# One windowed-attention kernel: transposed scores by tiles of keys, one slot later, with 8 KB stack rows loaded in three pieces

## The chip, the cores and the metric

The kernel runs on one core of one Trainium2 chip. The metric is the device time of one execution in microseconds (us). Below, PE is TensorE, DVE is VectorE, ACT is ScalarE, POOL is GpSimd and SP is SyncE, which here only issues transfers. "L786" is line 786 of the kernel before.

## The reference

Input `x` is 4 batches of 1024 tokens of width 256.

```python
h = layernorm(x) * (1 + ca) + sa                  # ca, sa, ... from silu(c) @ wmod, one row per batch
q, k, v = split(h @ qkv_w + qkv_b)                # 16 heads of 16
scores = q @ k.T / 4; allowed: 0 < key distance <= 128 (and key >= 0)
local = softmax(scores) @ v                       # a window of 128 keys before each query
rq = h @ rq_w + rq_b; rk, rv = split(mean over 16 tokens of h @ rkv_w + rkv_b)   # 4 latent heads
remote = softmax(rq @ rk.T / 4, earlier latents only) @ rv @ rout_w + rout_b
gate = sigmoid(local @ gl_w + remote @ gr_w)      # per head
x1 = x + ga * ((gate * local + (1 - gate) * remote) @ out_w + out_b)
h2 = layernorm(x1) * (1 + cb) + sb
out = x1 + gb * (layernorm(h2 + outs) * ln_g + ln_b)   # outs: attention over routed tokens
```

Both kernels, before and changed, leave out `outs` and compute `layernorm(h2)`; the change does not touch that branch.

## The kernel before

**Tiles and slots.** The 4096 tokens are 32 tiles of 128 (`NT = 32`), 8 to a batch (`NB = 8`). Every engine runs `slot(n)` for n = 0 to 34, and a slot works on several tiles at once, one stage each: A (layer norm and transpose) for tile n+4, P (projection of q or k for a pair of tiles) for n+3, Q (split into terms, stack) for n+2, K (v and latent projections) for n+1, S (scores by query rows, for the row maximum) for n, T (transposed scores, exp, mask, times v) for n-1, C (gate, output projection) for n-2, D (second branch, store) for n-3. The order inside a slot is written out by hand per engine in its `slot` function, and semaphores do the rest. On PE a slot opens with the transpose of the maxima at L786.

**Score precision and the stack.** q and k are float32 values that are split into three bf16 terms each. Six products of terms are summed by the matmul itself: `qst` holds, for each head, 6 blocks of 16 rows (terms 0,0,0,1,1,2 of q), `kst` the matching ones of k (terms 0,1,2,0,1,0), 96 rows in all. Rows 96 to 111 hold minus the row maximum (in `qst`) and a one-hot of the head (in `kst`), so that the transposed scores come out with the maximum already taken off. `shift` (ACT, L574) writes those 16 rows of `qst` for a tile.

**How a stack is made.** For a pair of tiles, the even tile's turn makes q and the odd tile's turn makes k. ACT, POOL, ACT, POOL compute the terms (`part1`, `res1`, `part2`, `part3`), then SP stores them to a DRAM scratch (`store_terms`, L345) and loads the stack back in 6 transfers of 16 partitions, 128 KB each (`load_stack`, L361), in pieces of 512 bytes. In slot n the terms are those of tile n+2, and the pair is first used by `scores` in the next even slot. So the k stack is stored and loaded in an odd slot and needed when the even slot after it starts: PE waits for `stack_loaded` at the head of `scores(t, 1)`, `t` even.

**SP's order.** In an odd slot SP issues: store of k terms, k stack loads, store of y. In an even slot: store of q terms, store of y (it waits for DVE's last operation of tile n-3), q stack loads. After slots 0, 2 and 4 it also issues 1 MB of `x` for the next batch (`load_batch`); `x_all` holds all of x.

**Transposed scores.** For query tile m = n-1 and each head, `scores_t` (L797, L798) runs two matmuls: queries of m against the keys of tile m-1 (not for a batch's first tile) and against those of m. Each loads its 128 keys as weights. ACT exponentiates two heads at a time (`exps`, L583), POOL masks four heads at a time (L432 own keys, L436 previous keys), and `sum_v` multiplies by v.

**Shared banks.** `project_v` (L731) writes the PSUM bank `p_qkv` that `shift` reads, and waits for it:

```python
pe.wait_ge(shift_ready, done(t - 2))
```

## Time and profile before

| | |
|---|---|
| median of 3 runs | 607.0 us (604.92 to 607.2) |
| the profiled execution's own time | 606.81 us |
| its span, first to last instruction | 605.1 us |
| busy: PE, DVE, ACT, POOL | 497.0, 433.6, 354.5, 378.3 us |
| mean granted clock of TensorE | 0.924 |
| packets of SP's transfer queue | 90428, 52.58 MB |

The span is what the trace accounts for; the 1.7 us around it lie outside. A change of 0.5% (3 us) is about what the measurement can tell. A matmul's own duration includes its way through the array, so the spacing of starts, not the duration, tells what a stream of matmuls costs.

### The profile page before, as it was taken

How to read it: one execution, taken by the hardware profiler on the slowest of the kernel's cores; microseconds unless marked ns; L12 is line 12 of the kernel's file. 1: busy time of each engine (PE TensorE's matmuls, PEld its weight loads, DVE VectorE, ACT ScalarE, POOL GpSimd, SP SyncE). 2: the span in 40 equal slices, each digit the busy share in tenths (PEclk: the TensorE clock that was granted, in tenths of full speed). 3: DMA queues.
4: the chain of work that ended last, by engine and by line, in shares of the span. 5: the costliest groups of instructions: out<-in, count | busy, mean ns of one | idle time of the engine just before them, and what ended most of it. 6: DMA issues, size and time to landing. Idle time of an engine off the chain costs nothing.

```text
span 605.1 us, 19951 instructions
## 1 busy us (share of the span) xinstructions
PE 497.0 (82%) x7168; PEld 373.3 (62%) x7168; DVE 433.6 (72%) x1193; ACT 354.5 (59%) x868; POOL 378.3 (63%) x516
## 2 busy tenths in 40 slices
PE   2547789897899979898989799998999798989771
PEld 2305567675677657676767577776776576756440
DVE  2255556787688868787879687886888786876645
ACT  1111467667477657676676657776776676654640
POOL 2313246777377647777777666775777575766652
PEclk9966899899799989999999988998999998997875
DMA  8487957529254755556282819183656565460000
GB/s 268 103 134 233 170 85 124 116 44 163 41 111 67 103 74 89 89 74 105 42 110 54 124 43 127 37 117 60 90 88 90 88 89 90 58 95 11 10 10 18
DMA packets 93388, 55.16 MB, mean 91 GB/s; under 512 B 8916, under 2 KB 91500, under 8 KB 93292
## 3 DMA queue, kind: packets, MB, share of 16 engines
q1 hardware_dynamic: 90428, 52.58, 51.3%
q10 hardware_dynamic: 2864, 1.31, 1.0%
q8 instruction: 59, 0.97, 0.8%
q14 instruction: 37, 0.30, 0.2%
HBM read 37.07 MB, written 16.80 MB: 89 GB/s over the span
## 4 chain that ended last, share of the span: by engine, by line
PE 67%; issue 16%; POOL 7%; DVE 4%; DMA 2%; ACTq 1%; SPq 1%; ACT 1%; POOLq 0%; DVEq 0%
PE p_qkv L721 9%; PE p_pv L810 8%; PE p_qkv L731 7%; PE p_misc L877 5%; PE p_x L776 5%; PE p_y L797 4%; PE p_x L769 4%; PE p_y L798 4%; PE p_a L742 2%; PE p_a L822 2%; PE p_misc L860 2%; PE p_qkv L851 2%; PE p_a L707 2%; PE p_a L744 2%; POOL pr L432 2%
## 5 line engine op out<-in xcount | busy, mean ns | idle before, releaser
L583 ACT ACTIVATE pr<-p_y 128x512 f32<-128x512 f32 x224 | 124.6, 595 | 66.1 <-PE p_y L798 63.8
L1150 DVE TENSOR_REDUCE mtok<-p_x 128x3 bf16<-128x480 f32 (+1 forms) x192 | 109.3, 585 | 60.5 <-PE p_x L776 54.3
L460 POOL TENSOR_TENSOR dif<-local,rem 128x272 f32<-128x272 f32 x32 | 30.9, 965 | 111.8 <-DVE local L1188 111.8
L432 POOL TENSOR_SCALAR_AFFINE_SELECT pr<-pr 128x512 f32<-128x512 f32 x128 | 89.6, 701 | 11.4 <-ACT pr L585 8.8
L442 POOL TENSOR_TENSOR rstd<-ve,half 128x1 f32<-128x1 f32 x96 | 58.3, 607 | 49.5 <-DVE ve L1070 49.4
L436 POOL TENSOR_SCALAR_AFFINE_SELECT pr<-pr 128x512 f32<-128x512 f32 x112 | 81.9, 731 | 0.0
L797 PE MATMUL p_y<-qst,kst 112*128 112x128 bf16 x448 | 67.2, 222 | 7.7 <-ACT pr L583 4.8
L798 PE MATMUL p_y<-qst,kst 112*128 112x128 bf16 x512 | 73.4, 221 | 0.0
L721 PE MATMUL p_qkv<-hT,wqk 128*128 128x256 f32 x256 | 67.7, 411 | 2.2 <-DVE qkf L1102 1.3
L810 PE MATMUL p_pv<-pr,vp 128*18 128x128 f32 x1920 | 68.4, 284 | 1.2 <-POOL pr L432 0.7
L769 PE MATMUL p_x<-edge,ident_bf 128*32 128x192 bf16 (+1 forms) x672 | 43.8, 250 | 28.5 <-issue 28.5
L810 PEld LDWEIGHTS p_pv<-pr,vp 128*18 128x18 f32 x1920 | 48.8, 101 | 19.4 <-POOL pr L436 9.6
L731 PE MATMUL p_qkv<-wv,hT 128*128 128x272 f32 x128 | 46.0, 491 | 18.0 <-issue 18.0
L574 ACT ACTIVATE qst<-p_qkv 16x2048 bf16<-16x2048 bf16 x32 | 59.8, 1870 | 0.8
L776 PE MATMUL p_x<-kst,qst 96*32 96x160 bf16 x1792 | 60.1, 238 | 0.0
L591 ACT ACTIVATE oT<-p_pv 128x512 f32<-128x512 f32 x32 | 19.1, 597 | 67.0 <-PE p_pv L810 67.0
L798 PEld LDWEIGHTS p_y<-qst,kst 112*128 112x128 bf16 x512 | 49.1, 99 | 10.2 <-issue 1.8
L721 PEld LDWEIGHTS p_qkv<-hT,wqk 128*128 128x128 f32 x256 | 49.4, 203 | 9.7 <-issue 2.2
L797 PEld LDWEIGHTS p_y<-qst,kst 112*128 112x128 bf16 x448 | 43.2, 99 | 17.9 <-issue 8.0
L416 POOL TENSOR_TENSOR qkf<-qkf,terms 128x512 f32<-128x512 f32 x32 | 40.2, 1258 | 18.2 <-ACT terms L562 18.1
L769 PEld LDWEIGHTS p_x<-edge,ident_bf 128*32 128x32 bf16 x672 | 17.9, 94 | 52.0 <-issue 43.7
L423 POOL TENSOR_TENSOR terms<-qkf,terms 128x512 bf16<-128x512 f32 x32 | 37.1, 1160 | 10.8 <-ACT terms L568 10.8
(131 smaller groups left out, 1104.5 us busy)
## 6 DMA issues: line engine op xcount, KB each, us to landing
qst<-scr_q SPq DMA_DIRECT2D x96, 128.0 KB, 4.8
kst<-scr_k SPq DMA_DIRECT2D x96, 128.0 KB, 4.4
scr_q<-terms SPq DMA_DIRECT2D x16, 384.0 KB, 2.8
scr_k<-terms SPq DMA_DIRECT2D x16, 384.0 KB, 6.4
out_y<-y SPq DMA_DIRECT2D x32, 128.0 KB, 2.0
x_all<-in_x SPq DMA_DIRECT2D x3, 1024.0 KB, 8.9
pr<-in_wmod SPq DMA_DIRECT2D x1, 1024.0 KB, 9.0
x_all<-in_x SPq DMA_DIRECT2D x1, 768.0 KB, 5.4
```

The lines of the kernel that those rows point to most:

```text
L432: ins = pool.affine_select(out=own, in_=own, compare_op=ALU.is_ge, fill=0.0, base=-1, pattern=[[0, 4], [1, P]], channel_multiplier=-1)
L436: ins = pool.affine_select(out=prev, in_=prev, compare_op=ALU.is_ge, fill=0.0, base=-1, pattern=[[0, 4], [-P, P]], channel_multiplier=P + 1)
L574: act.activation(q_of(t)[KS:KS + H, :, :], p_qkv[KS:KS + H, 0:P // 2].bitcast(BF16).unsqueeze(1).to_broadcast([H, H, P]), ACT.Copy).then_i ...
L583: act.activation(pr[:, 2 * i:2 * i + 2, :, :], src, ACT.Exp).then_inc(exp_done[i], 1)
L721: ins = pe.matmul(p_qkv[:, 2 * b * P:2 * (b + 1) * P], wqk[:, k, half * D + b * P:half * D + (b + 1) * P], hT[:, r:r + 2, k, :], start=(k ...
L731: ins = pe.matmul(p_qkv[:, 0:H * (HD + 1)], hT[:, t % 4, k, :], wv[:, k, :, :].rearrange("p h k -> p (h k)"), start=(k == 0), stop=(k == K ...
L769: pe.matmul(ends[g * QG:(g + 1) * QG], ident_bf[:, g * QG:(g + 1) * QG], edge[:, :].unsqueeze(1).to_broadcast([P, h1 - h0, 2 * QG]).rearra ...
L776: ins = pe.matmul(win[g * QG:(g + 1) * QG, h - h0, :], q_of(t)[0:KS, h, g * QG:(g + 1) * QG], keys[:, at:at + WIN], start=False, stop=True ...
L797: pe.matmul(p_y[i % 2][:, at:at + P], kst[0:KS + H, h, (n - 1) % NB, :], q, start=True, stop=True)
L798: ins = pe.matmul(p_y[i % 2][:, at + P:at + 2 * P], kst[0:KS + H, h, n % NB, :], q, start=True, stop=True)
L810: ins = pe.matmul(p_pv[32 * j:32 * j + VC, g * P:(g + 1) * P], vp[:, (n - 1 + a) % RING, h, :], pr[:, h, a, :], start=(a == 0 or n % NB == ...
L1150: dve.tensor_reduce(mtok[:, KS + h0:KS + h1], p_x[i % 2][:, 0:(h1 - h0) * w].rearrange("p (h n) -> p h n", n=w), AX_X, ALU.max, negate=Tru ...
```

## The change

Three things change together.

1. **Transposed scores go by key tile.** `scores_t(t)` now takes the keys of tile t as weights once per head and runs 256 columns of queries past them: those of tile t (own keys) and of tile t+1 (which sees them as previous keys). It needs the maxima and the stack of tile t+1, so the T stage moves one slot later, behind a new stage M (maxima, `shift`, latent output) that stays at n-1. T is then n-2, C is n-3, D is n-4, and there are 36 slots instead of 35. A batch's last tile has no next, so it is the last tile, not the first, that has half of the scores, exps and masks. `pr` gets a third part per head (own, and two that alternate for the previous keys), `vp` a fifth tile.
2. **Stack rows.** The host reorders the columns of q and k in `qkv_w`, so that in a term a partition is (element of the head, group of heads) and 8 partitions of 1 KB lie one behind the other in the scratch: one stack row, 8 KB, for all heads. The scratch of k is stored with its terms reversed. A stack is then loaded in 3 transfers (`RUNS`: 48, 32 and 16 rows) instead of 6 of 16 rows. `qst` holds all 8 tiles of a batch, `q_and_next` picks columns of two tiles, and the loads into it wait for the scores of tile r-7 rather than r-3.
3. **x in a ring.** To pay for the SBUF, `x_all` holds 16 tiles; the first 1 MB load stays behind slot 0, and then 4 loads of 4 tiles follow slots 7, 11, 15 and 19.

```diff
-Q_TERMS = (0, 0, 0, 1, 1, 2)
-K_TERMS = (0, 1, 2, 0, 1, 0)
+RUNS = ((0, 3), (1, 2), (2, 1))
+NRUN = len(RUNS)
...
-        qst = sb("qst", [P, 2, H, 2 * P], BF16)
+        qst = sb("qst", [P, NB // 2, H, 2 * P], BF16)
...
+        def q_and_next(t, h):
+
+            flat = qst[0:KS + H, :, :, :].rearrange("p b h n -> p (b h n)")
+            at = (t % NB // 2 * H + h) * 2 * P + t % 2 * P
+            if t % 2 == 0:
+                return flat[:, at:at + 2 * P].rearrange("p (r n) -> p r n", n=P)
+            step = 2 * H * P - P
+            if at + 2 * step <= NB * H * P:
+                return flat[:, at:at + 2 * step].rearrange("p (r n) -> p r n", r=2)[:, :, 0:P]
...
-                sp.dma_start(scr[half].rearrange("t p n -> p t n"), terms[:, half, :, :, :].rearrange("p s b n -> p (s b) n"))\
+                sp.wait_ge(stack_loaded[half], halves(r - 2, 16 * NRUN))
+                sp.dma_start(scr[half].rearrange("t p n -> p t n"), terms[:, half, :, :, :].rearrange("p s b n -> p s (b n)"))\
...
-                sp.wait_ge(st_psum[LAST_ST], done(r - (7 if half else 3)))
+                sp.wait_ge(st_psum[LAST_ST], done(r - 7))
...
-                for i in range(NTERM):
+                for skip, terms_in in RUNS:
+                    rows_ = terms_in * HD
+                    src = scr[half][skip:skip + terms_in] if half else scr[half][0:terms_in]
+                    src = src.rearrange("t (d g) n -> (t d) (g n)", d=HD)
                     if half:
-                        dst = kst[i * HD:(i + 1) * HD, :, n:n + 2, :].rearrange("d h r n -> d h (r n)")
+                        dst = kst[row0:row0 + rows_, :, n:n + 2, :].rearrange("d h r n -> d h (r n)")
+                        src = src.rearrange("d (h n) -> d h n", h=H)
                     else:
-                        dst = qst[i * HD:(i + 1) * HD, n // 2 % 2, :, :]
+                        dst = qst[row0:row0 + rows_, n // 2, :, :].rearrange("d h n -> d (h n)")
...
             def scores_t(t, i):
 
-                pe.wait_ge(shift_ready, done(t))
+                pe.wait_ge(shift_ready, done(t + 1 if has_next(t) else t))
...
-                    q = q_of(t)[0:KS + H, h, :]
-                    if n % NB:
-                        pe.matmul(p_y[i % 2][:, at:at + P], kst[0:KS + H, h, (n - 1) % NB, :], q, start=True, stop=True)
-                    ins = pe.matmul(p_y[i % 2][:, at + P:at + 2 * P], kst[0:KS + H, h, n % NB, :], q,
-                                    start=True, stop=True)
+                    keys = kst[0:KS + H, h, t % NB, :]
+                    if has_next(t):
+                        ins = pe.matmul(p_y[i % 2][:, at:at + 2 * P].rearrange("p (r n) -> p r n", n=P), keys, q_and_next(t, h),
+                                        start=True, stop=True)
+                    else:
+                        ins = pe.matmul(p_y[i % 2][:, at:at + P], keys, q_of(t)[0:KS + H, h, :], start=True, stop=True)
...
                 if T:
-                    scores_t(m, 1)
+                    scores_t(n, 1)
```

**SP, one pair of tiles in mid-program.** SP's rows from a store of y in an even slot to the next one, of the kernel before, with the semaphores that SP waits for:

```order
57 L366 DMA out_y<-y 128x256 [waits y_ready]
58 L361 DMA qst<-scr_q 16x16x256 [waits st_psum6,q_terms_stored]
59 L361 DMA qst<-scr_q 16x16x256 x5
60 L345 DMA scr_k<-terms 128x6x256 [waits k_stack_loaded,part3_ready]
61 L361 DMA kst<-scr_k 16x16x256 [waits st_psum6,k_terms_stored]
62 L361 DMA kst<-scr_k 16x16x256 x5
63 L366 DMA out_y<-y 128x256 [waits y_ready]
64 L345 DMA scr_q<-terms 128x6x256 [waits q_stack_loaded,part3_ready]
```

The same stretch of the changed kernel:

```order
75 L413 DMA out_y<-y 128x256 [waits y_ready]
76 L408 DMA qst<-scr_q 48x4096 [waits st_psum6,q_terms_stored]
77 L408 DMA qst<-scr_q 32x4096
78 L408 DMA qst<-scr_q 16x4096
79 L385 DMA scr_k<-terms 128x3x512 [waits k_stack_loaded,part3_ready]
80 L408 DMA kst<-scr_k 48x16x256 [waits st_psum6,k_terms_stored]
81 L408 DMA kst<-scr_k 32x16x256
82 L408 DMA kst<-scr_k 16x16x256
83 L413 DMA out_y<-y 128x256 [waits y_ready]
84 L377 DMA x_all<-in_x 128x4x256 [waits xb_ready]
85 L385 DMA scr_q<-terms 128x3x512 [waits q_stack_loaded,part3_ready]
```

The order of kinds is the same; six loads have become three, the pieces of a q row are 4096 elements long and those of a k row still 256, and in 4 of the odd slots a load of x stands behind the store of y.

**PE, the last slots.** PE's last rows of the kernel before: the end of slot 32 (the last with transposed scores, whose rows end just above), and slot 33:

```order
1804 L868 MATMUL p_misc<-cst,mix 128x128 x2
1805 L810 MATMUL p_pv<-pr,vp 18x128 x8
1806 L877 MATMUL p_misc<-wo,mixT 128x256 x2
1807 L810 MATMUL p_pv<-pr,vp 18x128 x24
1808 L860 MATMUL p_misc<-cst,oT 128x128 x4
1809 L868 MATMUL p_misc<-cst,mix 128x128 x2
1810 L877 MATMUL p_misc<-wo,mixT 128x256 x2
```

And of the changed kernel, the end of slot 32 (its first row below), slot 33 and slot 34:

```order
1035 L862 MATMUL p_pv<-pr,vp 18x128 x24
1036 L851 MATMUL p_y<-qst,kst 128x128 x2
1037 L912 MATMUL p_misc<-cst,oT 128x128 x4
1038 L851 MATMUL p_y<-qst,kst 128x128 x14
1039 L920 MATMUL p_misc<-cst,mix 128x128 x2
1040 L862 MATMUL p_pv<-pr,vp 18x128 x8
1041 L929 MATMUL p_misc<-wo,mixT 128x256 x2
1042 L862 MATMUL p_pv<-pr,vp 18x128 x24
1043 L912 MATMUL p_misc<-cst,oT 128x128 x4
1044 L920 MATMUL p_misc<-cst,mix 128x128 x2
1045 L929 MATMUL p_misc<-wo,mixT 128x256 x2
```

Between the two slots that the kernel before has there, the changed kernel has one more, with the last tile's 16 single matmuls of 128 columns, its `sum_v` and the output of the tile before.

## Rows read from the trace of the kernel before

**Rows 1.** The page: engine PE, and the chain that ended last.

```profile
PE 497.0 (82%) x7168; PEld 373.3 (62%) x7168; DVE 433.6 (72%) x1193; ACT 354.5 (59%) x868; POOL 378.3 (63%) x516
...
PE 67%; issue 16%; POOL 7%; DVE 4%; DMA 2%; ACTq 1%; SPq 1%; ACT 1%; POOLq 0%; DVEq 0%
```

**Rows 2.** Stretches (slots 1-31; single slots): length, engines' busy us, clock, DMA share, GB/s.

```profile
68.57:572.90 504.33, 446.57 (x6898) 340.67 (x6899) 390.08 (x1069) 333.62 (x822) 347.35 (x466) 0.96 0.54 85
147.67:169.97 22.30, 16.73 (x239) 12.91 (x235) 13.28 (x37) 11.36 (x27) 12.08 (x16) 0.85 0.36 54
200.50:214.35 13.85, 12.45 (x196) 9.10 (x192) 11.33 (x35) 9.35 (x27) 9.08 (x12) 1.00 0.96 126
280.37:299.09 18.72, 16.15 (x239) 12.27 (x236) 13.26 (x38) 11.33 (x27) 12.07 (x16) 0.91 0.17 40
380.08:395.46 15.38, 14.32 (x237) 11.06 (x233) 13.57 (x37) 11.32 (x27) 12.11 (x16) 1.00 0.12 37
539.22:557.93 18.71, 16.20 (x229) 11.26 (x226) 11.65 (x30) 9.43 (x23) 9.44 (x14) 0.82 0.08 17
572.90:588.50 15.60, 10.78 (x117) 7.10 (x113) 6.67 (x16) 7.98 (x14) 9.64 (x14) 0.78 0.03 9
```

**Rows 3.** Waits of the whole run: total us, times, longest.

```profile
PE p_x L769 <- issue: 28.5, 11, 5.6
...
PE p_qkv L731 <- issue: 18.0, 16, 2.2
...
PE p_x L761 <- issue: 4.6, 3, 2.1
```

**Rows 4.** Timeline of SP and PE around slot 14, which starts at 280.37.

```profile
264.15 2.87 SPq L361 DMA_DIRECT2D qst<-scr_q  x6
267.49 0.38 SPq L345 DMA_DIRECT2D scr_k<-terms  x1
274.21 2.76 SPq L361 DMA_DIRECT2D kst<-scr_k  x6
...
283.17 0.27 PE L769 MATMUL p_x<-edge,ident_bf 128*32 128x192 bf16 x4 [2.57 <-issue]
```

**Rows 5.** Transfers of the whole run: KB each, median us from issue to landing.

```profile
kst<-scr_k SPq DMA_DIRECT2D x96, 128.0 KB, 4.4
scr_q<-terms SPq DMA_DIRECT2D x16, 384.0 KB, 2.8
scr_k<-terms SPq DMA_DIRECT2D x16, 384.0 KB, 6.4
...
x_all<-in_x SPq DMA_DIRECT2D x1, 768.0 KB, 5.4
```

**Rows 6.** Stretches with one transfer: 768 KB of x, then a q stack.

```profile
24.00:25.50 1.50, 1.39 (x4) 0.68 (x2) 0.00 (x0) 0.17 (x1) 0.00 (x0) 1.00 1.09 343
...
268.00:271.50 3.50, 3.28 (x40) 2.45 (x44) 2.69 (x10) 3.17 (x14) 1.29 (x3) 1.00 1.20 111
```

**Rows 7.** PE's timeline: the first and the last of 8 transposed-score matmuls in a row.

```profile
256.36 0.23 PE L797 MATMUL p_y<-qst,kst 112*128 112x128 bf16 x1
...
256.76 0.22 PE L798 MATMUL p_y<-qst,kst 112*128 112x128 bf16 x1
```

**Rows 8.** Timeline of slot 13: ACT's `shift` and PE's `project_v`.

```profile
266.25 1.87 ACT L574 ACTIVATE qst<-p_qkv 16x2048 bf16<-16x2048 bf16 x1
...
268.22 1.16 PE L731 MATMUL p_qkv<-wv,hT 128*128 128x272 f32 x4 [0.83 <-issue]
```

**Rows 9.** PE's timeline of slot 32, which starts at 572.90, and of slot 33.

```profile
575.92 0.63 PE L860 MATMUL p_misc<-cst,oT 128*128 128x128 f32 x4
...
589.21 0.66 PE L860 MATMUL p_misc<-cst,oT 128*128 128x128 f32 x4 [0.73 <-ACT oT L591]
...
594.78 0.69 PE L868 MATMUL p_misc<-cst,mix 128*128 128x128 f32 x2 [4.92 <-DVE mix L1202]
...
595.94 2.07 PE L877 MATMUL p_misc<-wo,mixT 128*128 128x256 f32 x4 [0.47 <-ACT mixT L629]
```

More of the change, by code:

```diff
@@ L27 @@
 RING = 4
+VRING = 5
+XRING = 2 * NB
+XC = NB // 2
 QG = P // 4
@@ L272, in halves, with term, has_next, own_and_next @@
             return per * (t // 2 + 1 + Y_BASE)
+        def term(half, s):
+            return terms[:, half, 2 - s if half else s, :, :]
         def q_of(t):
-            return qst[:, t // 2 % 2, :, :].rearrange("p h (r n) -> p h r n", n=P)[:, :, t % 2, :]
+            return qst[:, t % NB // 2, :, :].rearrange("p h (r n) -> p h r n", n=P)[:, :, t % 2, :]
+        def has_next(t):
+            return t % NB < NB - 1
+        def q_and_next(t, h):
[6 more added lines that the diff above has]
+                return flat[:, at:at + 2 * step].rearrange("p (r n) -> p r n", r=2)[:, :, 0:P]
+            return flat[:, at - step + P:at + step + P].rearrange("p (r n) -> p r n", r=2)[:, :, step - P:step]
+        def own_and_next(t, h0, h1):
+            return pr[:, h0:h1, 0:2 + (t + 1) % 2:1 + (t + 1) % 2, :]
+        def prev_of(t, h0, h1):
+            return pr[:, h0:h1, 1 + t % 2, :]
+        def x_loads(t):
+            return 16 * (1 if t < XRING else (t - XRING) // XC + 2)
         def scale_wo(eng, b, setup_sem):
@@ L287, in stages_of @@
         def stages_of(n):
[L289 removed]
+            return "".join(c for c, t in zip("APQKSMTCD", range(n + LEAD, n - 5, -1)) if 0 <= t < NT)
         def run(slot):
[L292 removed]
+            for n in range(NT + 4):
                 slot(n, stages_of(n))
@@ L384, in _ @@
             store_rows()
-            for n in range(NT + 3):
+            for n in range(NT + 4):
                 slot(n, stages_of(n))
-                if n in (0, 2, 4):
-                    load_batch(n // 2 + 1)
+                if n == 0:
+                    load_second_batch()
+                t0 = n + 1 + NB
+                if t0 % XC == 0 and XRING <= t0 < NT:
+                    load_x(t0)
             for p in range(2):
@@ L415, in res1 @@
                 half = t % 2
-                pool.tensor_tensor(qkf[:, half, :, :], qkf[:, half, :, :], terms[:, half, 0, :, :], ALU.subtract)\
+                pool.tensor_tensor(qkf[:, half, :, :], qkf[:, half, :, :], term(half, 0), ALU.subtract)\
                     .then_inc(res_ready, 1)
@@ L422, in part3 @@
                 half = t % 2
-                pool.tensor_tensor(terms[:, half, 2, :, :], qkf[:, half, :, :], terms[:, half, 1, :, :], ALU.subtract)\
+                pool.tensor_tensor(term(half, 2), qkf[:, half, :, :], term(half, 1), ALU.subtract)\
                     .then_inc(part3_ready, 1)
@@ L561, in part1 @@
                 act.wait_ge(terms_stored[half], halves(t - 2, 16))
-                act.activation(terms[:, half, 0, :, :], qkf[:, half, :, :], ACT.Copy).then_inc(part1_ready, 1)
+                act.activation(term(half, 0), qkf[:, half, :, :], ACT.Copy).then_inc(part1_ready, 1)
             def part2(t):
@@ L567, in part2 @@
                 act.wait_ge(res_ready, done(t))
-                act.activation(terms[:, half, 1, :, :], qkf[:, half, :, :], ACT.Copy).then_inc(part2_ready, 1)
+                act.activation(term(half, 1), qkf[:, half, :, :], ACT.Copy).then_inc(part2_ready, 1)
             def shift(t):
                 act.wait_ge(mT_psum, done(t))
-                act.wait_ge(st_psum[LAST_ST], done(t - 4))
+                if t >= NB:
+                    act.wait_ge(st_psum[LAST_ST], done(t - NB))
                 act.activation(q_of(t)[KS:KS + H, :, :], p_qkv[KS:KS + H, 0:P // 2].bitcast(BF16).unsqueeze(1).to_broadcast([H, H, P]),
@@ L645, in slot @@
                 if T:
-                    exps(m, 1)
-                    exps(m, 0)
+                    exps(n, 1)
+                    exps(n, 0)
                 if A:
@@ L805, in sum_v @@
                 pe.wait_ge(oT_ready, done(t - 1))
-                n = t
-                for a in range(0 if n % NB else 1, 2):
+                first = 0 if t % NB else 1
+                for a in range(first, 2):
                     for j in range(4):
                         h = 4 * g + j
-                        ins = pe.matmul(p_pv[32 * j:32 * j + VC, g * P:(g + 1) * P], vp[:, (n - 1 + a) % RING, h, :],
-                                        pr[:, h, a, :], start=(a == 0 or n % NB == 0), stop=(a == 1),
+                        ins = pe.matmul(p_pv[32 * j:32 * j + VC, g * P:(g + 1) * P], vp[:, (t - 1 + a) % VRING, h, :],
+                                        pr[:, h, 0, :] if a else prev_of(t, h, h + 1)[:, 0, :], start=(a == first), stop=(a == 1),
                                         tile_position=(0, 32 * j))
@@ L929, in slot @@
                 if T:
-                    sum_v(m, 1)
+                    sum_v(n, 1)
                 if C:
```

145 lines of the change are left out of this document (75 added, 70 removed).

## The prediction

> **What bounds the kernel now.** I read the page first. PE is busy 82% of the span and holds 67% of the chain that ended last; 16% of the chain is "issue", time for which the profile names no releaser [rows 1]. So the work is PE's, and the question is what the idle stretches on PE are. The list of waits gives them: 28.5 us in 11 stretches before L769 and 4.6 us in 3 before L761, both the first matmuls of `scores(t, 1)`, and 18.0 us in 16 before L731 [rows 3]. The timeline says what the first kind is. SP begins the k stack loads at 274.21, PE could start slot 14 at 280.4 and starts its scores at 283.17, 2.57 us late [rows 4]; 4.4 us is the median landing of a k load and the last of the six is issued near 277 [rows 4, 5]. Nothing else that `scores(t, 1)` with even t waits for is late. These 33.1 us are waits for the k stack.
>
> The kind before L731 is `project_v` waiting for `shift`: ACT's 1.87 us from 266.25 end when L731 starts at 268.22 [rows 8]. The change leaves that as it is. It appears in the slots without a stack wait; where the stack is waited for, ACT gets ahead meanwhile.
>
> Then the slots, by PE's transpose at L786. A full slot without a stack wait takes 15.38 us at clock 1.00, a slot with half the T work 13.85, slot 14 with its wait 18.72 at clock 0.91, slot 6 22.30 at 0.85 [rows 2]. So 18.72 - 15.38 = 3.3 us is more than the 2.57 us of waiting, although the L731 wait of 0.83 drops out: the rest, about 1.6 us, is the lower clock that this slot shows after its idle time. Slots 1 to 31 take 504.33 us [rows 2]. Had none waited for its stack, they would be 25 full ones and 6 half ones (slots 8, 9, 16, 17, 24, 25): 25 x 15.38 + 6 x 13.85 = 467.6. **36.7 us hang on the k stack**, clock included.
>
> **The change part by part.**
>
> *The stack chain.* In slots 12 to 14 the k terms are stored from 267.49, the loads begin 6.7 us later, and PE goes on 9.0 us after that: 15.7 us from the store [rows 4]. PE needs the stack at 280.4 + 0.2, 13.1 us from the store. So the chain must become 2.6 us shorter. The parts: the k store takes 6.7 us, but the q store, same size, lands in 2.8, and medians say the same, 6.4 against 2.8 [rows 5]; the difference is that the k store stands behind the q stack's six loads, issued at 264.15 [rows 4]. A stretch with nothing but such a stack load moves 111 GB/s; 768 KB of x, the same bytes as one stack, move at 343 [rows 6]. Both keep the transfer engines busy. Stack loads fill 16 partitions each in 512-byte pieces, the x load all 128 in 1 KB pieces. The new loads stand between: 48, 32 and 16 partitions, q in 8 KB pieces, k still in 512-byte ones at its destination. The trace has no such load, so bounds. Store: 2.8 (q out of the way) to 6.7 (q as slow as now). Loads and first use: 5.4 (the x load from issue to landing [rows 5]) to 9.0 (as now). The chain is then 8.2 to 15.7 us; I take 3.5 for the store, since q gets both the longer pieces and the wider writes, and 7.0 for k, the middle of its bounds: 10.5, which is 2.6 us inside the 13.1. One such gain alone would do: with today's k load and the q store's 2.8, it is 11.8. So the stack waits go. The last four slots are already slow without it: slot 30 takes 18.71 at clock 0.82 [rows 2], since it has little work for PE; I leave 2 us of the excess there. Gain 36.7 - 2 = **34.7 us**. What stands next is PE itself, with the L731 wait: the full slot of 15.38 had DVE busy 13.57 and ACT 11.32, with all of them behind PE [rows 2].
>
> A page of the Trainium skill bears on this: "SBUF — State Buffer", section "Door 1: The DMA port swizzle", says that partitions 0 to 15 reach 4 ports and at most about 109 GB/s, 0 to 31 and 0 to 63 reach 8 and about 218. Behind the row of 111 GB/s the trace agrees. An estimate from that page: the three loads take 3.6 + 1.2 us for the wider two and up to 1.2 for the last, about 4.2 us in place of 7.2 if they follow each other (384, 256 and 128 KB); with it the chain would come to about 9, and the sum would stay the same.
>
> *Fewer, wider matmuls.* 8 transposed-score matmuls in a row start from 256.36 to 256.76, so one takes 57 ns for 128 columns, though each has new weights [rows 7]. At 2.4 GHz 128 columns are 53.3 ns. Two matmuls of 114 ns become one of 256 columns, 107 ns at least; 4 to 8 ns a head, 16 heads, 31 slots: 2 to 4 us. I take **2 us**; the bounds are 0 (a strided read of queries costs what the weights did) and 4. All of it lies on PE's path. The columns, ACT's exps and POOL's masks stay the same in number and size.
>
> The Trainium skill, "TensorE: Matmul & The Clock Gate", section "Back-to-back issue gap", gives 81 ns per matmul of 128 columns and 131 ns of 512 for sustained pairs of weight load and matmul. By that, an estimate of about 98 ns for 256 columns, each head would save 64 ns and all of them about 30 us. The row of 57 ns says that the weight loads are hidden here, and I go by the row; what the rule would make is the rival below.
>
> *One slot later.* Slot 1 loses the T work of tile 0, half of the usual: a half is 15.38 - 13.85 = 1.5 us [rows 2]. Slot 2 has tile 0's half `sum_v`. I take **2 us** off, bounds 0 (the k stack of slot 2 becomes what is waited for, as slot 1 is shorter) and 3. At the end stands a new slot with tile 31's half T and tile 30's output. Its bounds: slot 32 of before, 15.6 us [rows 2], and slot 33, where `mix` was alone, 594.78 - 588.5 = 6.3 us to its transpose and 3.2 more until the output matmuls end at 598.0 [rows 2, 9], 9.5. In slot 32 the tokens' transposes L860 begin 3.0 us after its start, in slot 33 0.7 [rows 9], because ACT has no `shift` there. The new slot has none either, so 15.6 - 2.3 = 13.3, and half the exps: **12.8 us**. Nothing covers this cost.
>
> *The rest.* The loads of x at slots 7, 11, 15 and 19 are 512 KB behind the store of y, over a full odd slot's k load, and in time for nothing: at x's 343 GB/s they take 1.5 us [rows 6], and the next transfer, the q store, comes 2.5 us into the next slot. If they were in a stack's way it would cost 1.5 us, four times. The 1 MB load after slot 4 goes, which is what made slot 6 22.30; that is in the 36.7. Looser waits (`qst`, `st_psum`) cost nothing.
>
> *The sum.* 606.8 - 34.7 - 2 - 2 + 12.8 = **580.9**, from the profiled execution's 606.81, which stands 0.2 below the median. I say 581.
>
> **The rivals.**
>
> *The stack becomes faster, but too little.* For: the k pieces stay at 512 bytes, and if the pieces and not the partitions make 111 GB/s, k gains nothing. Against: the q side alone is worth up to 3.9 us. If the chain falls to 14.3, 1.2 us of wait stay in 15 even slots, about 0.6 net of the L731 wait that then drops out: +9, **590 us**.
>
> *The loads are not faster at all.* Then the 36.7 stay but for slot 6's load of x (22.30 - 18.72 = 3.6), and the new last slot is paid: 606.8 - 3.6 - 4 + 12.8 = **612 us**, slower. It decides once the chain gains less than about 0.6 us per pair (15 pairs against the 8.8 us of added slot net of the rest). Against it: x's 343 GB/s.
>
> *Another engine bounds the slot.* With no stack wait DVE has 1.8 us free per slot [rows 2], and ACT writes and POOL masks one stage later; a late exp or mask of 0.5 us in each of 31 slots gives +15, **596 us**. Against: the full slot at 15.38 with none such.
>
> *The weight loads were not hidden.* By 64 rather than 4 ns a head: -28, **553 us**. Against: 57 ns [rows 7].
>
> **How the numbers follow.** Chances: stack wait gone 0.72, too little 0.10, another engine 0.09, loads not faster 0.06, weight loads 0.03. The prediction is the first: 581, its own range 574 to 588 by the bounds of the last slot (-3, +3), the matmuls (-2, +2), slot 1 and 2 (-1, +2) and the late slots (-2, +2), not all at once. The whole range takes in the case at 590 and half of the one at 596: 570 to 596. By 0.5% (3 us), what a measurement of this kernel can tell from no change: faster 0.91, same 0.03, slower 0.06.
>
> **What the profile would show.** Right: no wait over 0.5 us before the first matmul of an even slot; full slots of 15.2 to 15.4 at clock 1.00, odd and even alike; the k store landing in under 4 us; the stretch of a q stack load at 200 GB/s or more; q's packets of 8 KB; transposed-score matmuls 107 to 111 ns apart; one slot of 11 to 15 us more at the end. Wrong: a stack wait that stays, full slots over 15.6 with a wait for ACT or POOL in them, or a lower clock in slots that did not wait.

## The result, and the profile after

The changed kernel takes 585.06 us (581.81 to 588.12, 4 runs) against 606.82 us (604.92 to 607.2, 4 runs) before: a ratio of 0.9647, 95% interval 0.9581 to 0.9712. The forecast was 581, range 570 to 596. The profiled execution took 583.01 us for a span of 581.3, at a mean clock of 0.938.

The page, where it answers to [rows 1]: PE, the chain that ended last, and the group of the new transposed-score matmuls.

```profile
PE 483.7 (83%) x6720; PEld 352.0 (61%) x6720; DVE 436.1 (75%) x1193; ACT 354.9 (61%) x868; POOL 378.4 (65%) x516
...
PE 62%; issue 15%; POOL 9%; DVE 7%; DMA 4%; ACTq 1%; SPq 1%; ACT 1%; POOLq 0%; DVEq 0%
...
L848 PE MATMUL p_y<-qst,kst 112*128 112x256 bf16 x448 | 74.2, 277 | 8.8 <-ACT pr L634 4.8
```

Half of the scores' pairs became one: 448 fewer matmuls, and 448 fewer weight loads. DVE, ACT and POOL do what they did.

The waits of the whole run (total us, times, longest), against [rows 3]; L821 is the first matmul of `scores(n, 1)`, L783 is `project_v`.

```profile
PE p_qkv L783 <- issue: 28.3, 28, 2.2
...
PE p_x L821 <- issue: 4.1, 7, 1.1
```

The stack waits fell from 33.1 us to 4.1. The wait for `shift` before `project_v` rose from 18.0 us in 16 slots to 28.3 in 28: it had been absent only in slots that had waited for their stack.

Stretches, against [rows 2] (length, engines' busy us, clock, DMA share, GB/s): slots 1 to 31, then slots 1, 2, 8, 13, 14, 32, the new slot 33, and the last two.

```profile
67.74:537.42 469.68, 427.44 (x6376) 315.97 (x6376) 387.15 (x1053) 330.44 (x811) 341.66 (x457) 0.98 0.42 90
67.74:80.56 12.82, 9.88 (x134) 6.63 (x135) 7.97 (x21) 6.01 (x17) 2.82 (x3) 0.87 0.81 174
80.56:97.75 17.19, 13.76 (x182) 9.59 (x183) 8.17 (x24) 10.16 (x25) 8.54 (x12) 0.80 0.28 70
174.26:189.35 15.09, 13.65 (x164) 10.65 (x160) 12.88 (x38) 11.12 (x27) 11.41 (x16) 1.00 0.23 76
248.84:264.12 15.28, 14.40 (x224) 10.89 (x220) 13.49 (x37) 11.37 (x27) 12.10 (x16) 1.00 0.75 140
264.12:279.40 15.28, 14.47 (x223) 10.91 (x220) 13.25 (x37) 11.37 (x27) 12.10 (x16) 1.00 0.11 37
537.42:552.30 14.88, 10.91 (x103) 6.70 (x99) 6.67 (x16) 8.08 (x15) 8.66 (x13) 0.77 0.03 10
552.30:564.70 12.40, 8.10 (x89) 5.03 (x88) 5.94 (x16) 3.62 (x11) 6.50 (x10) 0.72 0.04 12
564.70:581.30 16.60, 3.42 (x10) 1.88 (x10) 7.91 (x25) 1.21 (x3) 4.38 (x6) 0.59 0.05 16
```

A full odd slot and a full even one now take the same 15.28 us at clock 1.00: the alternation of 15.38 and 18.72 is gone. Slots 1 to 31 went from 504.33 to 469.68 at 0.98, and one slot of 12.40 us was added.

The chain that the prediction timed, as in [rows 4], for slot 14, which starts at 264.12: SP's issues and PE's first scores.

```profile
248.09 1.32 SPq L408 DMA_DIRECT2D qst<-scr_q  x3
251.34 0.38 SPq L385 DMA_DIRECT2D scr_k<-terms  x1
256.51 1.91 SPq L408 DMA_DIRECT2D kst<-scr_k  x3
...
264.52 0.27 PE L821 MATMUL p_x<-edge,ident_bf 128*32 128x192 bf16 x4 [0.17 <-issue]
```

Issue of the k store to issue of the k loads 5.2 us (it was 6.7), and from there to PE's first scores 8.0 (it was 9.0): 13.2 in place of 15.7, and PE waits 0.17 us. The chain ends as PE arrives, with no room. From the end of SP's issue of the k loads to PE's first scores it is 6.1 us (it was 6.2). The transfers, against [rows 5] (KB each, median us to landing):

```profile
scr_q<-terms SPq DMA_DIRECT2D x16, 384.0 KB, 2.5
qst<-scr_q SPq DMA_DIRECT2D x16, 384.0 KB, 4.6
scr_k<-terms SPq DMA_DIRECT2D x16, 384.0 KB, 4.7
kst<-scr_k SPq DMA_DIRECT2D x16, 384.0 KB, 5.5
```

The k store still lands 2.2 us later than the q store of the same size, and it is still the one with a stack load issued some 3 us ahead of it, 3.25 us in the rows above.

By stretches of the two profiled executions: the start is 0.8 us shorter, slots 1 and 2 unchanged (30.02 and 30.01), slots 3 to 31 shorter by 34.6 (474.31 and 439.67), the rest from slot 32 on longer by 11.7 (32.18 and 43.88). Together 23.8 us less.

### The profile page after: what moved, and what is told of

The parts are those of the page before. It is cut to its first block, busy times and chain, and to the rows that moved or that the text cites. A ratio compares the mean times of both kernels' runs of the same rounds, so it can differ in the third digit from the quotient of the medians.

```text
span 581.3 us, 18955 instructions
## 1 busy us (share of the span) xinstructions
PE 483.7 (83%) x6720; PEld 352.0 (61%) x6720; DVE 436.1 (75%) x1193; ACT 354.9 (61%) x868; POOL 378.4 (65%) x516
## 4 chain that ended last, share of the span: by engine, by line
PE 62%; issue 15%; POOL 9%; DVE 7%; DMA 4%; ACTq 1%; SPq 1%; ACT 1%; POOLq 0%; DVEq 0%
PE p_pv L862 8%; PE p_qkv L773 8%; PE p_y L848 7%; PE p_qkv L783 6%; PE p_misc L929 5%; PE p_x L828 4%; PE p_x L821 4%; POOL pr L482 2%; PE p_a L794 2%; PE p_qkv L903 2%; PE p_a L874 2%; PE p_misc L912 2%; PE p_a L759 2%; POOL pr L486 2%; PE p_a L796 2%
## 5 line engine op out<-in xcount | busy, mean ns | idle before, releaser
L482 POOL TENSOR_SCALAR_AFFINE_SELECT pr<-pr 128x512 f32<-128x512 f32 x128 | 89.8, 703 | 10.6 <-ACT pr L634 9.6
L848 PE MATMUL p_y<-qst,kst 112*128 112x256 bf16 x448 | 74.2, 277 | 8.8 <-ACT pr L634 4.8
L773 PE MATMUL p_qkv<-hT,wqk 128*128 128x256 f32 x256 | 65.0, 399 | 2.2 <-DVE qkf L1155 1.3
L783 PE MATMUL p_qkv<-wv,hT 128*128 128x272 f32 x128 | 40.1, 439 | 28.3 <-issue 28.3
L848 PEld LDWEIGHTS p_y<-qst,kst 112*128 112x128 bf16 x448 | 39.5, 98 | 29.4 <-issue 12.6
L773 PEld LDWEIGHTS p_qkv<-hT,wqk 128*128 128x128 f32 x256 | 48.1, 198 | 10.1 <-issue 2.2
L821 PE MATMUL p_x<-edge,ident_bf 128*32 128x192 bf16 (+1 forms) x672 | 43.5, 248 | 4.4 <-issue 4.1
L783 PEld LDWEIGHTS p_qkv<-wv,hT 128*128 128x128 f32 x128 | 23.3, 202 | 36.5 <-issue 33.4
L473 POOL TENSOR_TENSOR terms<-qkf,terms 128x512 bf16<-128x512 f32 x32 | 36.9, 1154 | 10.6 <-ACT terms L618 10.5
L602 ACT ACTIVATE hT<-p_a,mod_t 128x128 f32<-128x128 f32 x64 | 25.8, 452 | 29.5 <-PE p_a L759 29.5
L929 PE MATMUL p_misc<-wo,mixT 128*128 128x256 f32 x128 | 40.6, 444 | 0.9 <-ACT mixT L680 0.5
```

The source lines that it names most:

```text
L482: ins = pool.affine_select(out=own, in_=own, compare_op=ALU.is_ge, fill=0.0, base=-1, pattern=[[0, 4], [1, P]], channel_multiplier=-1)
L773: ins = pe.matmul(p_qkv[:, 2 * b * P:2 * (b + 1) * P], wqk[:, k, half * D + b * P:half * D + (b + 1) * P], hT[:, r:r + 2, k, :], start=(k ...
L783: ins = pe.matmul(p_qkv[:, 0:H * (HD + 1)], hT[:, t % 4, k, :], wv[:, k, :, :].rearrange("p h k -> p (h k)"), start=(k == 0), stop=(k == K ...
L821: pe.matmul(ends[g * QG:(g + 1) * QG], ident_bf[:, g * QG:(g + 1) * QG], edge[:, :].unsqueeze(1).to_broadcast([P, h1 - h0, 2 * QG]).rearra ...
L848: ins = pe.matmul(p_y[i % 2][:, at:at + 2 * P].rearrange("p (r n) -> p r n", n=P), keys, q_and_next(t, h), start=True, stop=True)
L929: ins = pe.matmul(p_misc[:, 0:D], mixT[:, k * P:(k + 1) * P], wo[:, (t // NB * KC + k) * D:(t // NB * KC + k + 1) * D], start=(k == 0), st ...
```

## The experiments

Four kernels beside one of before (611.11 us, 13 runs), then three kernels and a transfer program beside another (608.98, 7 runs), then two (607.84, 7 runs). Times are compared by ratio to the kernel before of the same group; stretches are those of profiled executions. "Slot n" starts with PE's transpose of the maxima, as before.

### The loads without the later slot: e1_loads_only

The kernel before with part 2 of the change alone: the column order, the scratch, the three loads. T stays at n-1 with two matmuls per head, `qst` holds two pairs, and x comes in loads of 1 MB.

```diff
-                for i in range(NTERM):
+                for skip, terms_in in RUNS:
+                    rows_ = terms_in * HD
...
-                        dst = kst[i * HD:(i + 1) * HD, :, n:n + 2, :].rearrange("d h r n -> d h (r n)")
+                        dst = kst[row0:row0 + rows_, :, n:n + 2, :].rearrange("d h r n -> d h (r n)")
...
-                        dst = qst[i * HD:(i + 1) * HD, n // 2 % 2, :, :]
+                        dst = qst[row0:row0 + rows_, n // 2 % 2, :, :].rearrange("d h n -> d (h n)")
```

> The kernel before with part 2 of the change alone: new column order, scratch by terms, stacks in three loads; T stays at n-1, x is loaded as before. Theory 1 (the gain is all in the loads, the later slot is a cost): the stack waits of 33 us go, full slots are 15.4, and the end has no extra slot of 12.4, so the profiled time is 583 - 12.4 + 2 (no wider matmuls) + 1.5 (tile 0's half in slot 1) = 574 us, 3 us more if the 1 MB load of x after slot 4 still delays slot 6. Theory 2 (moving T one slot later is what frees the slot, the loads alone do little): 600 us or more, with waits of 1 to 2.5 us left at the even slots.

Measured: 576.4 us (572.02 to 581.64), ratio 0.9441 (0.9363 to 0.952). Its interval lies wholly below that of the full change. Its stretches, slots 3 to 31 and the rest:

```profile
96.61:538.81 442.20, 403.60 (x6481) 309.50 (x6478) 374.75 (x1021) 313.91 (x770) 332.09 (x445) 1.00 0.42 88
538.81:570.30 31.49, 14.70 (x127) 9.78 (x123) 14.59 (x41) 9.08 (x17) 13.34 (x20) 0.66 0.04 13
```

Against the changed kernel: start 66.67 and 67.74, slots 1 and 2 29.94 and 30.01, slots 3 to 31 442.2 and 439.67, the rest 31.49 and 43.88. So the whole gain is in the loads. What the changed kernel has beyond them gives back 2.5 us in the middle and costs 12.4 at the end. The 2.5 is a balance. e1 still has the 1 MB load of x behind slot 4, and its slot 6 has 2.5 us of stack wait and takes 17.09 us against 15.29; its slot 3 is 2.0 longer too; and its slots 30 and 31 are 3.2 us shorter, at clock 1.00 where the changed kernel has 0.89 and 0.79. At the front it moves time without saving any: slot 1 falls from 14.66 to 12.82 and slot 2 rises from 15.28 to 17.19.

### Six narrow loads with long pieces: e2_six_loads

The changed kernel, its stack loaded again in 16 rows at a time from the same scratch: pieces of q stay 8 KB, those of k 512 bytes.

```diff
-RUNS = ((0, 3), (1, 2), (2, 1))
+RUNS = ((0, 1), (1, 1), (2, 1), (1, 1), (2, 1), (2, 1))
+Q_AT = (0, 1, 2, 0, 1, 0)
...
-                    src = scr[half][skip:skip + terms_in] if half else scr[half][0:terms_in]
+                    at = skip if half else Q_AT[i]
+                    src = scr[half][at:at + terms_in]
```

> The changed kernel with its stacks loaded in six transfers of 16 rows instead of three, the pieces as they are (8 KB for q, 512 bytes for k). Theory 1 (the width of a load, 16 partitions, makes it slow): q and k stacks both move at about 110 GB/s again, the stack waits of 2.5 us come back in 14 even slots, some 583 + 33 = 616 us. Theory 2 (the piece size does it): q stays as quick as in the changed kernel, only k slows or not even that, and the time is 583 to 595 us.

Measured: 626.8 us (617.66 to 628.5), ratio 1.0208 (1.0086 to 1.0331). The ratio is that of its two shorter runs, 617.66 and 625.64, and the profile is of one of the two longer ones, 627.97; so how much slower it is stays less sure than that nothing is gained. The waits:

```profile
PE p_x L823 <- issue: 28.3, 11, 3.2
...
PE p_x L815 <- issue: 7.0, 3, 2.5
```

35.3 us of stack wait against 33.1 before the change. The long pieces alone take none of it away. They act on both sides: the k store lands in 5.4 us, a microsecond sooner than the 6.4 of before, and a k load now in 5.2 where it was 4.4. What sets the changed kernel apart from this one is that a load covers up to 48 partitions, and with it that there are three loads instead of six.

### Two matmuls per head: e3_two_matmuls

The changed kernel with `scores_t` as two matmuls of 128 columns for each head, same order of work.

```diff
-                        ins = pe.matmul(p_y[i % 2][:, at:at + 2 * P].rearrange("p (r n) -> p r n", n=P), keys, q_and_next(t, h),
-                                        start=True, stop=True)
+                        for r in range(2):
+                            ins = pe.matmul(p_y[i % 2][:, at + r * P:at + (r + 1) * P], keys, q_of(t + r)[0:KS + H, h, :],
+                                            start=True, stop=True)
```

> The changed kernel with two matmuls of 128 columns per head and key tile in scores_t instead of one of 256; same columns, twice the weight loads. Theory 1 (weight loads are hidden at 57 ns a matmul): 2 to 3 us slower than the changed kernel, some 0.07 to 0.1 us a slot. Theory 2 (two weight loads and matmuls cost 81 ns each): full slots about 1 us longer, 610 us or more.

Measured: 583.78 us (581.16 to 587.6), ratio 0.9591 (0.9518 to 0.9665): no difference from the changed kernel that the times can tell. The same slot as above, 13:

```profile
247.64:263.02 15.38, 14.54 (x239) 11.28 (x235) 13.58 (x37) 11.33 (x27) 12.11 (x16) 1.00 0.70 139
```

15.38 against 15.28. So the wide matmul is worth 0.10 us a full slot, 6 ns a head; an estimate from that is 2 to 2.5 us over the program, and slots 3 to 27 are 2.4 us longer here than in the changed kernel. Here the second matmul of a head has the same keys as weights, loaded anew; e1, where they differ, has the same 15.39 in most of its full slots.

### The old loads in the later slot: e4_old_loads

The changed kernel with the six loads of 512-byte pieces, the scratch and the column order of before; parts 1 and 3 stay.

```diff
-RUNS = ((0, 3), (1, 2), (2, 1))
+Q_TERMS = (0, 0, 0, 1, 1, 2)
+K_TERMS = (0, 1, 2, 0, 1, 0)
...
-                        dst = qst[row0:row0 + rows_, n // 2, :, :].rearrange("d h n -> d (h n)")
+                        dst = qst[i * HD:(i + 1) * HD, n // 2, :, :]
```

> The changed kernel with part 2 undone: column order, scratch and six 512-byte loads per stack as before; T one slot later, x in a ring, wide matmuls stay. Theory 1 (the later slot costs, the loads gain): the stack waits come back, 583 + 33 (about 31 without slot 6's load of x) - 1 = 610 to 616 us, slower than the kernel before by 4 to 9 us. Theory 2 (the later slot or the looser waits carry the gain): 590 us or less.

Measured: 613.29 us (10 runs; nine lie between 608.11 and 620.61, one took 1093.19, unexplained), ratio 1.0028 (0.9971 to 1.0086). The waits, and slots 3 to 31:

```profile
PE p_x L817 <- issue: 24.8, 11, 3.2
...
PE p_x L809 <- issue: 6.4, 3, 2.6
```

```profile
102.23:565.95 463.72, 411.83 (x6065) 305.88 (x6062) 368.29 (x1009) 314.60 (x770) 328.98 (x443) 0.97 0.54 83
```

Without the new loads nothing is gained: this is the rival "the loads are not faster". The prediction's 612 against 606.8 is a ratio of 1.0086, at the upper end of this interval. The stack waits are back with 31.2 us, and the end costs its 12 us (44.0 from slot 32 on, against 32.2). That the time is level all the same comes from slots 3 to 31: they take 463.7 us against 474.3 before, 10.6 us less. So with the old loads parts 1 and 3 do give back nearly what the end costs; slot 6, without the 1 MB load of x, has 3.8 of it, the matmuls some 2.5, and the rest is not taken apart. Within the changed kernel the loads are worth 24.0 us in slots 3 to 31 (463.7 and 439.7) and 0.7 in slots 1 and 2. Another 3.7 lie before slot 1, but there the profiled executions differ among each other: 68.6 us before the change with the old loads, 70.2 in e6 with the new ones.

### The transfers by themselves: e5_loads_alone

A program with nothing but transfers, of which there is one execution; what it puts out is a copy of x, and nothing of the reference is computed. Each group is waited for before the next is issued. All stack loads bring the same 768 KB into 96 partitions; they differ in how many partitions one covers (six of 16; 48, 32 and 16; two of 48; one of 96) and in their pieces: `q` 512 bytes in the scratch and in SBUF, `k` 8 KB in the scratch and 512 bytes in SBUF, `q8k` 8 KB in both.

```python
for rows in (NARROW, WIDE, HALVES, ONE):
    group(*[(q512[a:a + w, :, 0, :], small[:, a:a + w, :].rearrange("h r n -> r h n")) for a, w in rows])
    group(*[(k512[a:a + w, :, 0:2, :].rearrange("r h a n -> r h (a n)"),
             stack[a:a + w, :].rearrange("r (h n) -> r h n", h=H)) for a, w in rows])
    group(*[(q8k[a:a + w, :], stack[a:a + w, :]) for a, w in rows])
```

> Transfers alone, one group after the other, with nothing else on the core; the output is a copy of x and nothing of the reference is computed. Each stack load of 768 KB is made in four splits (six of 16 rows, 48 + 32 + 16, two of 48, one of 96) and in three kinds of pieces (512 bytes at both ends, 8 KB at the source and 512 bytes in SBUF, 8 KB at both ends), and the terms of 384 KB are stored in pieces of 512 bytes and 1 KB. Theory 1 (the number of partitions that are written at once sets the rate): six of 16 take about 7 us of transfer whatever the piece, 48 + 32 + 16 about 4 to 4.5, and 96 rows at once 2.5 to 4. Theory 2 (the pieces set the rate): 512-byte pieces take 7 us in each split, 8 KB pieces under 4 in each.

SP's timeline, the second pass; from a row's start to the next row's start is the group's time, issue, landing and SP's waking included.

```profile
122.48 2.79 SPq L45 DMA_DIRECT2D q<-small  x6
131.48 3.81 SPq L45 DMA_DIRECT2D k<-stack  x6
140.88 2.63 SPq L45 DMA_DIRECT2D q8k<-stack  x6
148.52 1.42 SPq L45 DMA_DIRECT2D q<-small  x3
155.24 1.91 SPq L45 DMA_DIRECT2D k<-stack  x3
162.60 1.25 SPq L45 DMA_DIRECT2D q8k<-stack  x3
168.97 0.89 SPq L45 DMA_DIRECT2D q<-small  x2
175.04 1.24 SPq L45 DMA_DIRECT2D k<-stack  x2
181.34 0.79 SPq L45 DMA_DIRECT2D q8k<-stack  x2
187.03 0.32 SPq L45 DMA_DIRECT2D q<-small  x1
192.87 0.55 SPq L45 DMA_DIRECT2D k<-stack  x1
198.73 0.32 SPq L45 DMA_DIRECT2D q8k<-stack  x1
```

Differences of the starts, in us:

| loads | q | k | q8k |
|---|---|---|---|
| six of 16 rows | 9.0 | 9.4 | 7.6 |
| 48, 32, 16 | 6.7 | 7.4 | 6.4 |
| two of 48 | 6.1 | 6.3 | 5.7 |
| one of 96 | 5.8 | 5.9 | |

From six loads to three with the same pieces: 9.0 to 6.7, 9.4 to 7.4, 7.6 to 6.4. From 512 bytes at both ends to 8 KB at both, with the same widths: 1.4 us less with six loads, 0.4 with three. An 8 KB source with 512-byte writes, which is what k has now, is slower than 512 bytes at both ends, by 0.4 us with six loads and 0.6 with three. So q goes from 9.0 to 6.4, of which the wider loads are 2.3; k goes from 9.0 to 7.4, all of it by the wider loads, with 0.6 given back by the pieces. (The q of the kernel before lies in one piece of 8 KB in SBUF; a load with 512-byte pieces in the scratch alone is not among these.)

In this table the loads become wider and fewer together, and SP's issue becomes shorter with their number: 2.79 to 1.42 us for q, 3.81 to 1.91 for k, about as much as k's group gains. Shorter issue is not all of it, since the data are still moving when the issue is over: with six q loads at 104 GB/s over the 4.5 us after it (125.3 to 129.8), with three at 180 GB/s over the 4.0 us after it (150.0 to 154.0). But whether the rate comes from the width of a load or from the number of loads no run here tells apart; all that is shown is that fewer and wider loads of the same bytes are quicker.

The stores of 384 KB, alone, take 2.76 us in pieces of 512 bytes and 2.53 in pieces of 1 KB, from the start of their issue to that of the next group.

### ACT's shift first: e6_shift_first

e1 with ACT's order changed: `part2` and `shift` come before `out_t`, which waits for work of PE's late in the slot before. It aims at the wait before `project_v`, which is what e1 has left.

```diff
                 if Q:
                     part1(r)
-                if C:
-                    out_t(c)
                 if Q:
                     part2(r)
                 if T:
                     shift(m)
+                if C:
+                    out_t(c)
+                if T:
                     lat_oT(m)
```

> The kernel before with the new loads (as the run with the loads only, T at n-1), and on ACT part2 and shift ahead of out_t. Theory 1 (project_v waits for shift, which stands behind out_t on ACT): the wait of 0.83 to 1.3 us before it falls by about 0.6 to 0.9 in 28 slots, 572 - 20 = 550 to 556 us, and the k store starts up to 0.9 us earlier in its slot. Theory 2 (project_v waits for something else, the copy of q or k in DVE): its wait stays and the time stays within 3 us of the run with the loads only, or is longer because out_t is late.

Measured: 569.18 us (562.16 to 572.39), ratio 0.931 (0.9226 to 0.9394). The waits:

```profile
PE p_x L778 <- issue: 12.1, 9, 3.4
...
PE p_qkv L740 <- issue: 5.4, 9, 2.1
...
PE p_x L770 <- issue: 1.5, 2, 0.9
```

`project_v` waits 5.4 us instead of e1's 28.4, but the stack waits are back with 13.6 (L778 and L770) against e1's 4.9. A slot of 14.5 us gives the chain 0.8 us less room, and it had none to spare. The mean clock of the profiled execution fell from e1's 0.958 to 0.937.

### The q loads ahead of y: e7_q_load_early

The changed kernel, where SP issues the q stack loads right behind the q store. The store of y, which has to wait for DVE's last operation of a tile, comes after them.

```diff
-                if Q and t % 2:
+                if Q:
                     load_stack(r)
                 if D_:
                     store(d)
-                if Q and t % 2 == 0:
-                    load_stack(r)
```

> The changed kernel with SP's q stack loads ahead of the store of y in even slots, right behind the q store. Theory 1 (the k store is late because it queues behind the q stack's data): the k store's median landing falls from 4.7 to the q store's 2.5 us, the k loads start 2 us earlier, the waits of 0.2 to 1.1 us that are left before some even slots go, and the time falls by 2 to 4 us at most, since the chain already fits the slot but for 1 us here and there. Theory 2 (the k store is slow by itself): it still lands in 4.5 us and nothing moves.

Measured: 582.28 us (580.35 to 583.51), ratio 0.9562 (0.9508 to 0.9616). SP's timeline in slot 13:

```profile
246.81 0.36 SPq L413 DMA_DIRECT2D out_y<-y  x1
250.52 0.38 SPq L385 DMA_DIRECT2D scr_k<-terms  x1
253.06 1.91 SPq L408 DMA_DIRECT2D kst<-scr_k  x3
```

The loads follow the store by 2.5 us instead of 5.2, and the median landing of the k store falls from 4.7 to 2.5, the q store's own. So the q stack in front of it was the whole difference, as the prediction had read from the stores of before. PE's stack wait is 0.8 us in all, in slot 2. Yet a full slot stays 15.28, because its other wait stands: `project_v` (L781) waits for `shift`, 32.0 us in all. Beside the changed kernel's 0.9647 the gain can't be told from nothing.

### Both orders: e8_both_orders, e9_later_both_orders and e10_old_loads_both_orders

e6 and e7 had each taken away one of two waits and met the other. e8 is e1 with both edits of order, e9 the changed kernel with both, e10 the kernel before, with its old loads, with both.

> The kernel before with the new loads, ACT's new order and SP's q loads ahead of the store of y. Theory 1: with shorter slots (14.5 us) the chain of k store and loads, 13.1 us in the changed kernel, no longer fits behind the k terms' place in the slot unless the q stack is out of its way, so this is 3 to 10 us faster than the run with ACT's order alone, 545 to 552 us. Theory 2 (part2's earlier place is enough): no difference between the two above 2 us.

Measured: 550.99 us (549.63 to 553.11), ratio 0.9053 (0.9009 to 0.9096). Its slot 13:

```profile
242.40:256.91 14.51, 14.51 (x240) 11.29 (x236) 13.25 (x38) 11.06 (x28) 12.08 (x16) 1.00 0.59 115
```

PE is busy for 14.51 of 14.51 us at clock 1.00, and over the whole run the waits are 1.6 us for the stack and 8.8 before `project_v`. By the ratios, from e1's 0.9441 to 0.9053, the two orders save some 24 us of 609; the ACT order alone saved 8 (0.9441 to 0.931, with intervals that overlap a little). The SP order alone was run only on the changed kernel, where e7 saved 5 (0.9647 to 0.9562), which overlapping intervals don't tell from nothing; on e1 it was not run.

> The changed kernel (T one slot later, wide matmuls, new loads) with ACT's new order and SP's early q loads. Theory 1 (the later slot costs its extra slot of 12 us at the end and gives back 2 to 3 us by wide matmuls, whatever the rest): full slots of 14.4 us and 551 + 12 - 3 + 2 (slot 2) = 560 to 563 us. Theory 2 (the later slot leaves room that pays once the slots are short): 550 us or less.

Measured: 559.77 us (559.26 to 561.29), ratio 0.9228 (0.9153 to 0.9303). Its last slots, from 32 on:

```profile
513.79:558.10 44.31, 23.27 (x201) 13.86 (x197) 20.53 (x57) 12.57 (x28) 19.57 (x29) 0.66 0.04 13
```

Against e8's 32.20 from slot 32 on, that is 12.1 us, the later slot's price again. It gets back 4.1 us over slots 3 to 31 (415.62 against e8's 419.69), slots 1 and 2 lose 0.6 and the start 1.6; by the spans 10.2 us remain. Its full slots take 14.50 or 14.51, as e8's do, so the wide matmuls give these nothing that shows.

> The kernel before with its six 512-byte loads, and only ACT's new order and SP's early q loads. Theory 1 (a q stack takes 9 us by six loads; issued 10.5 us into an even slot of 14.5 it still runs when the k store comes, so the k chain stays too long): stack waits of 1 to 2.5 us remain in the even slots, 570 to 585 us. Theory 2 (the order of the transfers alone was the trouble, not their speed): no stack waits, 550 to 556 us.

Measured: 583.37 us, the median of four runs of which one took 1090.3, again without a trace; the other three lie between 579.79 and 586.55, ratio 0.9592 (0.9484 to 0.97). The waits:

```profile
PE p_x L768 <- issue: 20.2, 9, 4.3
...
PE p_x L760 <- issue: 2.8, 2, 1.6
```

With the old loads both orders leave 23 us of stack wait. By the ratios 0.9592 and 0.9053 the new loads are worth 33 us once the orders are changed, about as much as in the old order (1 and 0.9441, 34).

## Why the prediction was right, and where its terms were off

*The stack waits: right in what they were, sized 2.4 us too high.* e4 and e1 show it from both sides: old loads in the new order of work 613.29, new loads in the old order 576.4. The prediction took 34.7; slots 3 to 31 gave 34.6, of which the matmuls carry 2 to 2.5 (e3), so the stack gave some 32.3, with the late slots in it. The step that failed is "25 full ones and 6 half ones". The half slot of 13.85 [rows 2] is slot 9, with the transposed scores of a batch's first tile. I took slots 8, 16 and 24 to be like it, and they are not: in the kernel before they hold those of a batch's last tile, all 32 matmuls where slot 9 has 16. In e1, slots 8 and 9, and the waits before `project_v` in them:

```profile
177.21:192.31 15.10, 13.80 (x181) 11.15 (x177) 12.93 (x39) 11.14 (x27) 11.42 (x16) 1.00 0.12 39
192.31:206.15 13.84, 12.44 (x196) 9.10 (x193) 11.34 (x35) 9.35 (x27) 9.08 (x12) 1.00 0.77 148
...
180.45 1.16 PE L739 MATMUL p_qkv<-wv,hT 128*128 128x272 f32 x4 [1.24 <-issue]
...
195.55 1.16 PE L739 MATMUL p_qkv<-wv,hT 128*128 128x272 f32 x4 [1.27 <-issue]
```

Both wait for `shift`, and slot 8 has 1.36 us more of PE's work. Before the change slot 8 took 15.13 with 1.3 us of stack wait; it takes 15.09 in the changed kernel and 15.10 in e1 without one, since the wait for `shift` came in its place. Three such slots, 1.24 each, are 3.7 us too much. That the term was off by only 2.4 leaves 1.3 us in small differences of many slots, which I can't assign. The late slots came near what was taken, but not by its reason: slot 30 of before, the row of 18.71 at clock 0.82, had 1.4 us of stack wait, so it was not slow "without it". Slots 28 to 31 of the changed kernel, with 15.28, 15.45, 16.25 and 15.93, are 1.8 us over four full ones; in e1, with its last two slots at clock 1.00, they are 1.8 us under four of 15.38. So the 2 us left there depend on the clock of the one execution, and that part was luck.

*The chain: 13.2 us, not 10.5.* The prediction took 3.5 for the store and 7.0 for the loads up to PE's first scores; they are 5.2 and 8.0. The store: the faster q loads should have been out of its way, and were not. e7, where nothing is in its way, has 2.5. The loads: alone they take 7.4 (e5). The estimate missed what is left of the queue, and the chain fits the 13.1 of room only just, where 2.6 us of margin had been reckoned: waits of 0.2 to 1.1 us stay in 7 slots. The 2.5 us that it did gain is about what SP's issue lost, 1.55 us for q's loads and 0.85 for k's. That the total came right with 13.2 in the place of 10.5 is luck, since PE waits for the stack only once the chain passes 13.1. The waits that stay are the rival "too little faster" at its edge, 4.1 us in place of the 18 (1.2 in 15 slots) that it stood for. That "one such gain alone would do" could not be had: with narrow loads the k store landed in 5.4 us, with long pieces for q (e2) and with q's narrow loads issued 6.0 us ahead of it instead of 3.3 (e10) alike. Two signs that the prediction had set for itself failed: no wait over 0.5 us before an even slot's first matmul (five of the seven are longer), and the k store landing in under 4 us (4.7). Slot 31, with no stack wait and clock 0.79, is one of its signs of being wrong. Its sign of 200 GB/s came for q's loads (229 from 249 to 251) and not for k's (169 from 258.5 to 262.5).

The Trainium skill, "SBUF — State Buffer", section "Door 1: The DMA port swizzle", has loads into few partitions bound by the ports that these reach. e5 agrees in direction: the same 768 KB take 9.0, 6.7, 6.1 and 5.8 us as six loads of 16 rows, as three of 48, 32 and 16, as two of 48 and as one of 96. By the estimate from its figures the three would save 3.0 us (7.2 to 4.2; the 4.2 needs 1.8 for the 384 KB of the first load at 218 GB/s, and the prediction's 3.6 is a slip). Measured are 2.3 and 2.0, issue and landing included, in groups that differ in the number of loads as well.

*Fewer, wider matmuls: right.* 2 us, measured 0.10 us a slot. e1 has two matmuls per head with different weights, and its full slots between 4 and 29 without a stack wait are 15.28 to 15.47; by the rule of the Trainium skill's "TensorE: Matmul & The Clock Gate", section "Back-to-back issue gap", weighed as a rival at 64 ns a head, they would be a microsecond longer than the changed kernel's 15.28. The rival falls, as the row of 57 ns had it.

*Slots 1 and 2: no gain, where 2 us were taken.* The bound of 0 had its reason in the text, the k stack of slot 2, and it was a part of it. PE's rows of slot 2:

```profile
80.56 0.23 PE L838 MATMUL p_qkv<-ident_bf,mtok 128*128 128x128 bf16 x1 [0.77 <-DMA kst<-scr_k]
...
81.61 0.27 PE L821 MATMUL p_x<-edge,ident_bf 128*32 128x192 bf16 x4 [0.81 <-issue]
...
84.66 2.15 PE L783 MATMUL p_qkv<-wv,hT 128*128 128x272 f32 x4 [0.92 <-issue]
...
96.97 0.85 PE L862 MATMUL p_pv<-pr,vp 128*18 128x128 f32 x24 [1.60 <-POOL pr L486]
```

That is 3.3 us of waiting within slot 2, of which 0.81 is for the stack and 0.92 for `shift`, and its clock is 0.80. The 1.60 before `sum_v` is POOL's last mask, with too little other work left for PE in front of it. In e3 the same slot has 3.2 us of waits and takes 15.93 at clock 0.89, with 12.68 us of PE busy in place of 13.76; so about a microsecond of the 17.19 goes with the clock. Why e3's clock is higher there stays open: e7 (17.18) and e9 (17.51) have waits of the same size in it.

*The last slot: 12.40, predicted 12.8.* Slot 32 became 14.88 from 15.60, which the sum had not costed, and the last stretch is as it was, 16.60 us. e9 against e8 gives 12.1 for the same thing.

*The other rivals.* In the middle no slot waits for another engine beyond the wait for ACT's `shift`, which was there before. The 512 KB loads of x cost nothing that shows: 15.28 in slots 13 and 14 as elsewhere.

The sum, predicted and then measured: stack 34.7, and some 32.3; matmuls 2, and 2 to 2.5; slots 1 and 2 2, and 0; the end 12.8, and 11.7; not foreseen, 0.8 less before slot 1. Together 25.9 us less were predicted and 23.8 measured.

## What to carry to other kernels

Three edits came together, and the one that carries all the gain needs neither of the others: time each part by itself before paying for a later stage with 12 us. A wait that covers a second wait hides its price; before adding up slots without the first, ask of each kind of slot whether the second then stands there, and try the edits for both together, since here ACT's order alone gave 8 us, SP's order alone (on the changed kernel) 5 that noise could make, and both on e1 gave 24. Several small loads into few partitions should be joined into one that covers many, before their pieces are made longer.
